# Attention values by token: transposes of the queries in place of a second projection

## What is computed

```python
qkv = x @ Wqkv_w.T + Wqkv_b
q = qkv[..., :nf]                      # nf = 192, 12 heads of 16
q = q.reshape(nb, ns, N_HEADS, hd).transpose(0, 2, 1, 3)
k = q
v = q
w = jnp.einsum('bhqd,bhkd->bhqk', q, k) * (1.0 / jnp.sqrt(jnp.float32(hd)))
mask = jnp.tril(jnp.ones((ns, ns), dtype=x.dtype))
w = jax.nn.softmax(w * mask - NEG_BIG * (1.0 - mask), axis=-1)
a = jnp.einsum('bhqk,bhkd->bhqd', w, v)
return a.transpose(0, 2, 1, 3).reshape(nb, ns, nf) @ Wproj_w.T + Wproj_b
```

## Time and profile before

| | us |
|---|---|
| median of three runs | 5412.71 |
| lowest, highest | 5407.25, 5437.77 |
| the profiled execution | 5446.25 |
| its span | 5444.5 |
| PE busy in it | 4705.0 (86%) |
| attention phase in it, about | 26 to 986 |

### The profile page before, as it was taken

One profiled execution on the slowest core, in us unless ns is written; L12 is line 12 of the kernel. 1 busy time (PEld: TensorE's weight loads), 2 busy tenths in 40 slices (PEclk: granted clock), 3 DMA queues, 4 the chain that ended last, 5 costly groups with the idle time before them and its releaser, 6 DMA issues. The chain is left out here.

```text
span 5444.5 us, 60695 instructions
## 1 busy us (share of the span) xinstructions
PE 4705.0 (86%) x16744; PEld 2469.9 (45%) x16744; DVE 3409.2 (63%) x4887; ACT 2337.0 (43%) x3842; POOL 3170.8 (58%) x1554
## 2 busy tenths in 40 slices
PE   5999999649959999999999898999899850899993
PEld 3777777326623433334434343434334320566662
DVE  2454544401119999999999999999999950111113
ACT  1333333302126566666666655566566530122220
POOL 2121111232219999999999898999899937222220
PEclk7999999869979999999999999999999975999996
DMA  4000000033312333332323232232233202333335
GB/s 192 16 15 12 15 15 6 13 94 120 104 45 97 103 105 104 104 103 101 105 96 112 88 102 97 98 107 96 97 100 105 90 13 77 117 112 114 114 113 166
DMA packets 239869, 473.51 MB, mean 87 GB/s; under 512 B 37324, under 2 KB 145180, under 8 KB 237692
## 3 DMA queue, kind: packets, MB, share of 16 engines
q1 hardware_dynamic: 216316, 424.11, 24.0%
q0 software_dynamic: 23424, 48.10, 2.5%
HBM read 399.02 MB, written 73.09 MB: 87 GB/s over the span
## 5 line engine op out<-in xcount | busy, mean ns | idle before, releaser
L1605 POOL TENSOR_TENSOR m_xh<-m_u,m_Bb 128x1536 f32<-128x1536 f32 x512 | 1760.9, 3467 | 203.4 <-DVE m_u L1483 203.4
L1534 PE MATMUL bank<-m_xh,ident 128*128 128x512 f32 x3072 | 1448.7, 607 | 24.6 <-POOL m_xh L1594 24.6
L1561 ACT ACTIVATE bank<-m_dt,m_Ac 128x508 f32<-128x508 f32 x1536 | 1020.9, 683 | 464.3 <-DVE bank L1576 310.0
L1576 DVE TENSOR_TENSOR_SCAN bank<-bank,m_xh 128x512 f32<-128x512 f32 x864 | 1059.5, 1226 | 34.1 <-ACT bank L1561 7.8
L1534 PEld LDWEIGHTS bank<-m_xh,ident 128*128 128x128 f32 x3072 | 570.8, 192 | 808.6 <-issue 730.9
L1594 POOL TENSOR_TENSOR m_xh<-m_xh,m_Cb 128x1536 f32<-128x1536 f32 x224 | 773.1, 3452 | 8.8 <-DVE m_xh L1576 8.8
L1576 DVE TENSOR_TENSOR_SCAN m_xh<-bank,m_xh 128x512 f32<-128x512 f32 x672 | 771.3, 1203 | 7.0 <-POOL m_xh L1605 3.6
L1585 DVE TENSOR_TENSOR m_xh<-bank,m_Cb 128x512 f32<-128x512 f32 x864 | 597.6, 692 | 66.8 <-DMA m_Cb<-BC_rows 21.2
L1017 POOL DMA_INDIRECT rows_y<-f1t_y,f1t_home x156 | 150.5, 965 | 565.2 <-DVE f1t_y L1046 527.7
L368 DVE TENSOR_REDUCE mx<-bank 128x3 f32<-128x384 f32 x256 | 142.3, 556 | 440.3 <-PE bank L535 439.2
L438 ACT ACTIVATE S<-S 128x384 f32<-128x384 f32 x256 | 133.9, 523 | 585.6 <-DVE S L370 585.6
(11 more groups left out here) (293 smaller groups left out, 6327.9 us busy)
## 6 DMA issues: line engine op xcount, KB each, us to landing
m_Bb<-BC_rows SPq DMA_DIRECT2D x256, 512.0 KB, 4.7
m_Cb<-BC_rows SPq DMA_DIRECT2D x256, 512.0 KB, 3.9
f1t_w<-f_w SPq DMA_DIRECT2D x39, 576.0 KB
slots_x<-zeros SPq DMA_DIRECT2D x12, 1254.5 KB, 31.1
f1t_x<-slots_x SPq DMA_DIRECT2D x39, 386.0 KB, 3.7
f1t_w1a<-f_w SPq DMA_DIRECT2D x39, 384.0 KB
f1c_yg<-rows_y SPq DMA_DIRECT2D x16, 768.0 KB, 4.7
f0t_w<-f_w SPq DMA_DIRECT2D x19, 576.0 KB, 4.4
```

The costliest lines, as they stand in the source:

```text
L1534: mm = pe.matmul(bank[:, c, :], K.ident[:, :], xh[n % NX][:, c, :], start=False, stop=(d == 1 and n == NS - 1))
L1561: act.activation(o[:, :, lo:hi], seqs(dt[d][:, c, :])[:, :, lo:hi], ACT.Exp, scale=Ac[:, c, n:n + 1]).then_inc(s_dA, 1)
L1576: dve.tensor_tensor_scan(o, bank[:, 3 + p % 3, way], xh[n % NX][:, c, way], 0.0, ALU.mult, ALU.add).then_inc(s_h, 1)
L1605: pool.tensor_tensor(xh[n % NX][:, :, :], u[d][:, :, :], Bb[q % RB][:, n % QN, :].unsqueeze(1).to_broadcast([P, DC, TOK]), ALU.mult).then_ ...
```

## The change

`V` is no longer computed by a second projection. The bias row of the padded weights gets a 1.0 in column 16 of each head, so that `qT` has a row of ones beside each head's 16 rows; transposing `qT` then gives the values, the ones column and the zeros at once. The projection has seven steps: k = 0, 1, 2 as before, and k = 3 to 6 one for each sequence, three 128x128 transposes of `qT` each, and one ScalarE copy of 128x384 each. k = 3 waits for all three copies of `qT`. The steps stand at other units. The weights `wq_a`, `wq_b` with their three loads go, and so do the four memsets of `V`; GpSimd gets one memset (twelve elements in one partition).

```diff
--- before.py
+++ after.py
@@ -143,7 +143,6 @@
         ds_t = sb("ds_t", [66, C])
         gam, bet = sb("gam", [P, C]), sb("bet", [P, C])
         wqp_a, wqp_b = sb("wqp_a", [P, HC * P]), sb("wqp_b", [CR + 1, HC * P])
-        wq_a, wq_b = sb("wq_a", [P, C]), sb("wq_b", [CR + 1, C])
         wo_a, wo_b = sb("wo_a", [P, C]), sb("wo_b", [CR + 1, C])
         mask = sb("mask", [P, HC, P], BF16)
         col_i = sb("col_i", [P, 2], I32)
@@ -184,7 +183,8 @@
         s_qps, s_q = sem("qps_ready"), sem("q_ready")
         s_sc, s_mx, s_sub, s_exp = sem("scores_ready"), sem("max_ready"), sem("sub_ready"), sem("exp_ready")
         s_pT, s_pTc, s_pv = sem("probsT_ready"), sem("probsT_copied"), sem("pv_ready")
-        s_OT, s_O, s_V = sem("heads_copied"), sem("heads_back"), sem("V_cleared")
+        s_OT, s_O = sem("heads_copied"), sem("heads_back")
+        NQ = HC + G
         s_ri, s_at, s_aT, s_aTc = sem("rowsum_inv"), sem("att_ready"), sem("attT_ready"), sem("attT_copied")
         s_pr, s_out = sem("proj_ready"), sem("res_ready")
 
@@ -203,20 +203,17 @@
                 pool.memset(mask[:, :, :], 0.0).then_inc(cleared, 1)
                 pool.iota(col_i[:, :], pattern=[[0, 2]], base=0, channel_multiplier=1).then_inc(cleared, 1)
                 pool.wait_ge(cleared, 4)
+                pool.memset(wqp_b[CR:CR + 1, :].rearrange("p (h x) -> p h x", x=32)[:, :, HD:HD + 1], 1.0).then_inc(cleared, 1)
+                pool.wait_ge(cleared, 5)
                 pool.affine_select(out=mask[:, :, :], in_=mask[:, :, :], compare_op=ALU.is_ge,
                                    fill=-4.0 * BIG, base=0, pattern=[[0, HC], [-1, P]], channel_multiplier=1).then_inc(cleared, 1)
-                pool.wait_ge(cleared, 5)
+                pool.wait_ge(cleared, 6)
                 pool.iota(col_i[64:128, 1:2], pattern=[[0, 1]], base=0, channel_multiplier=1).then_inc(cleared, 1)
-                pool.wait_ge(cleared, 6)
+                pool.wait_ge(cleared, 7)
                 pool.tensor_copy(col[:, :], col_i[:, :])
 
             @block.vector
             def _(dve):
-                for v in V:
-                    dve.memset(v[:, :, :, :], 0.0).then_inc(s_V, 1)
-                dve.wait_ge(s_V, 2)
-                for v in V:
-                    dve.memset(v[:, :, :, HD:HD + 1], 1.0)
                 dve.memset(zeros[:, :, :], 0.0).then_inc(s_zeros, 1)
                 dve.memset(mul3[:, :], 3.0).then_inc(mul3_set, 1)
                 dve.memset(zTb[CR:CR + 1, :], 1.0)
@@ -231,8 +228,6 @@
                 for dst, src in (
                     (posi_t[:, :], A["posi_table"]), (ds_t[0:64, :], A["demo_table"]), (ds_t[64:66, :], A["seg_table"]),
                     (gam[:, :], A["ln_gamma"].partition_broadcast(P)), (bet[:, :], A["ln_beta"].partition_broadcast(P)),
-                    (wq_a[:, :], A["WqkvT"][0:P, 0:C]), (wq_b[0:CR, :], A["WqkvT"][P:C, 0:C]),
-                    (wq_b[CR:CR + 1, :], A["bqkv"][0:1, 0:C]),
                     (wqp_a[:, :].rearrange("p (h x) -> p h x", x=32)[:, :, 0:HD],
                      A["WqkvT"][0:P, 0:C].rearrange("k (h d) -> k h d", d=HD)),
                     (wqp_b[0:CR, :].rearrange("p (h x) -> p h x", x=32)[:, :, 0:HD],
@@ -409,7 +404,7 @@
                 every_group(dve, dve_body)
 
 
-            Q_AT = {11: (0, 1), 13: (2, 3), 15: (4,)}
+            Q_AT = {11: (0, 1), 12: (2,), 14: (3, 4), 15: (5, 6)}
 
             def act_keep(act, g):
                 act.wait_ge(s_h1, g + 1)
@@ -417,7 +412,7 @@
 
             def act_zT(act, g):
                 if not isinstance(g, int) or g > 0:
-                    act.wait_ge(s_qps, g * 5)
+                    act.wait_ge(s_qps, g * NQ)
                 act.wait_ge(s_zTps, g * 2 + 1)
                 act.copy(zTa[:, :], bank[:, 6, :]).then_inc(s_zT, 1)
                 act.wait_ge(s_zTps, g * 2 + 2)
@@ -425,13 +420,11 @@
 
             def act_q(act, g, i, k):
 
-                act.wait_ge(s_qps, g * 5 + k + 1)
+                act.wait_ge(s_qps, g * NQ + k + 1)
                 if k < HC:
                     act.copy(qT[i][:, k, :], bank[:, 6 + k % 2, :]).then_inc(s_q, 1)
                 else:
-                    b = k - HC
-                    act.copy(V[i][:, 2 * b:2 * b + 2, :, 0:HD],
-                             bank[:, 6 + k % 2, 0:2 * C].rearrange("p (j h d) -> p j h d", j=2, h=HEADS)).then_inc(s_q, 1)
+                    act.copy(V[i][:, k - HC, :, :], bank[:, 6 + k % 2, 0:HC * P].rearrange("p (h d) -> p h d", h=HEADS)).then_inc(s_q, 1)
 
             def act_exp(act, g, u):
                 act.wait_ge(s_sub, g * UN + u + 1)
@@ -463,7 +456,8 @@
                     tile(act_OT, act, g, u, LC)
                     tile(act_aT, act, g, u, LA)
                     if u == 0 and not first(g):
-                        act_q(act, g, i, HC + 1)
+                        for k in Q_AT[UN - 1]:
+                            act_q(act, g, i, k)
                     if nxt is not None:
                         if u == 7:
                             act_keep(act, nxt)
@@ -477,7 +471,7 @@
             def _(act):
                 act_keep(act, 0)
                 act_zT(act, 0)
-                for k in range(HC + 2):
+                for k in range(NQ):
                     act_q(act, 0, 0, k)
                 every_group(act, act_body)
 
@@ -486,7 +480,7 @@
                 later = not isinstance(g, int) or g > 0
                 pe.wait_ge(s_onehot, g * 2 + 2)
                 if later:
-                    pe.wait_ge(s_q, g * 5)
+                    pe.wait_ge(s_q, g * NQ)
                 for b in range(2):
                     for j in (2 * b, 2 * b + 1):
                         o = bank[:, 6 + b, (j % 2) * C:(j % 2 + 1) * C]
@@ -505,28 +499,26 @@
                     mm = pe.transpose(bank[0:CR, 7, j * P:(j + 1) * P], z[:, j, P:C], K.ident[:, :])
                 mm.then_inc(s_zTps, 1)
 
-            def pe_q(pe, g, k):
+            def pe_q(pe, g, k, i):
                 if k == 0:
                     pe.wait_ge(s_zT, g * 2 + 2)
                 if k >= 2:
-                    pe.wait_ge(s_q, g * 5 + k - 1)
+                    pe.wait_ge(s_q, g * NQ + max(k - 1, HC if k == HC else 0))
                 if k < HC:
                     o = bank[:, 6 + k % 2, :]
                     pe.matmul(o, wqp_a[:, k * P:(k + 1) * P], zTa[:, :], start=True, stop=False)
                     pe.matmul(o, wqp_b[:, k * P:(k + 1) * P], zTb[:, :], start=False, stop=True).then_inc(s_qps, 1)
                 else:
-                    for j in (2 * (k - HC), 2 * (k - HC) + 1):
-                        o = bank[:, 6 + k % 2, (j % 2) * C:(j % 2 + 1) * C]
-                        sl = slice(j * P, (j + 1) * P)
-                        pe.matmul(o, zTa[:, sl], wq_a[:, :], start=True, stop=False)
-                        mm = pe.matmul(o, zTb[:, sl], wq_b[:, :], start=False, stop=True)
+                    j = k - HC
+                    for c in range(HC):
+                        mm = pe.transpose(bank[:, 6 + k % 2, c * P:(c + 1) * P], qT[i][:, c, j * P:(j + 1) * P], K.ident[:, :])
                     mm.then_inc(s_qps, 1)
 
             def pe_scores(pe, g, u, i):
                 j, r = u // RG, u % RG
                 n = g * UN + u
                 if u == 0:
-                    pe.wait_ge(s_q, g * 5 + HC)
+                    pe.wait_ge(s_q, g * NQ + HC)
                 if u >= 2 or not isinstance(g, int) or g > 0:
                     pe.wait_ge(s_sub, n - 1)
                 pe.matmul(bank[:, u % 2, 0:HC * P], K.identb[:, :], mask[:, :, :], start=True, stop=False)
@@ -548,8 +540,8 @@
                 j, r = u // RG, u % RG
                 n = g * UN + u
                 pe.wait_ge(s_pTc, n + 1)
-                if r == 0 and j % 2 == 0:
-                    pe.wait_ge(s_q, g * 5 + HC + j // 2 + 1)
+                if r == 0:
+                    pe.wait_ge(s_q, g * NQ + HC + j + 1)
                 if r == 0 and (j >= 2 or not isinstance(g, int) or g > 0):
                     pe.wait_ge(s_out, g * G + j - 1)
                 for c in range(HC):
@@ -595,14 +587,14 @@
                             pe_zT(pe, nxt)
                         elif u in Q_AT:
                             for k in Q_AT[u]:
-                                pe_q(pe, nxt, k)
+                                pe_q(pe, nxt, k, 1 - i)
 
             @block.tensor
             def _(pe):
                 pe_embed(pe, 0)
                 pe_zT(pe, 0)
-                for k in range(HC + 2):
-                    pe_q(pe, 0, k)
+                for k in range(NQ):
+                    pe_q(pe, 0, k, 0)
                 every_group(pe, pe_body)
```

## The result

The changed kernel took 5509.78 us (median of 22 runs, 5461.67 to 5558.73); the kernel before, measured beside it, 5454.96 us (22 runs). The ratio is 1.0098, with a 95% interval from 1.0069 to 1.0127: slower by 1%, or some 54 us. Every ratio here leaves out the few runs that lie over 1.5% above the fastest of their kernel, so it is not exactly the quotient of the two medians. The forecast was a ratio of 1.0035.

What follows compares the result with a forecast made beforehand. TensorE was taken to bound the attention phase; 5446.25 - 5.4 (start) + 24.2 (waits net of saved work) = 5465.1 us, factor 1.0035, applied to the 5412.71 us median: 5431 us. Own range 5412 to 5445; 8 in 10, 5389 to 5475.

Steps and rivals of the forecast that it cites:

- The bound, and 15 counts: Attention phase: TensorE is the bound, busy 137.02 of 140 us; the projections of groups 1 to 15 count 15 times.
- The start: Clears and loads before attention: without V's memsets 3.92 us and wq's loads 1.48 us, all that follows comes 5.40 us earlier.
- PE work: Projection steps: four transpose blocks, 1.52 us, replace 2.72 us of matmuls; gain 1.20 us per group, 18.0 us for 15.
- The hypothetical that the transposes are held at 1.2 GHz: New transpose blocks cost up to 3.04 us per group in place of 1.52; the gain becomes a loss, 5 us in all.
- The waits: PE waits for ScalarE copies, 1.03 us at u = 12 and 1.73 at u = 15; net +1.61 us per group, +24.2 us.
- Rival (a): The two copy waits are absorbed or not there: 5389 us without them, 5413 if absorbed; chance 0.18 for both.
- Rival (b), the clock: Clock falls in the u = 15 gap: 5509 us at one fall per group, 5440 to 5470 in a few; chance 0.17.
- the other row: Tail of the attention phase, 983 to 986 us: PE busy 1.20 of 3 us, next microsecond granted 0.80 on average.
- The price of a fall: Until the embedding at u = 1, two units take up to twice the time: 5.2 us per group, 78 us in all.
- The sum: Profiled execution: 5446.25 - 5.4 + 24.2 = 5465.1 us, a factor of 1.0035.
- The median: Whole kernel: the three runs' median, 5412.71 us, times the factor 1.0035 gives 5431.4 us.

Runs made afterwards that it cites:

- experiment 1: Changed kernel with ScalarE's qT and V copies at u = 12 and u = 15 put ahead of exp: ratio 0.9950, a second time 0.9948.
- the run with the long wait: Changed kernel with u = 15 copies early and the u = 12 wait lengthened to 2.1 us by two extra ScalarE copies: ratio 1.0034, again 1.0117.
- experiment 2: Changed kernel with only the copies at u = 12 ahead of exp, the wait at u = 15 left: ratio 1.0074.
- experiment 3: Changed kernel with only the copies at u = 15 ahead of exp, the wait at u = 12 left: ratio 0.9965.

## Why the prediction was wrong

- *The bound, and 15 counts*: right. The PE bounds the phase, and the waits stand 15 times each in the list.
- *The start*, -5.4 us: the mechanism right, mis-sized. 4.30 us at the slot clears, 3.52 where the PE waits for them, 2.1 at the `zTa` copy of group 1, behind the later rise of the clock. The forecast took the two parts as if nothing else in the chain moved.
- *PE work*, -1.20 us a group: right. By the starts of the rows a pair of blocks takes 0.71 and 0.77 us, 1.48 for the four against 2.72 before, a gain of 1.24. The period without the waits is 54.7 against 56.17 us, 1.4 to 1.5 less; what gives the other 0.2 was not looked for. The hypothetical that the transposes are held at 1.2 GHz, for which the prediction named the Trainium skill (TensorE: Matmul & The Clock Gate, Part 4: PE-mode transpose), did not come: experiment 1 ran them at 1.00.
- *The waits*, 1.03 and 1.73 us, +1.61 net: right. Measured in the same way 1.09 and 1.74, and +1.60. Reading where each copy stands in ScalarE's order, behind which exp, gave this to a few hundredths; the busy share of ScalarE (38% of the phase) would have given nothing.
- *Rival (a)*: refuted, no part of the waits was absorbed.
- *Rival (b), the clock*: this is the step that failed. The sum put the cost of the clock at nothing, where the runs show about 32 us. The rival had the place (the wait at u = 15), the direction and the rows, but a chance of 0.17, and most of that for "a few groups". The argument against it, "1.00 throughout from 160 to 300 us with the same transposes", compared a stretch without such idle spells with one that gets a spell of 1.7 us per group, and so was no argument. "A gap alone does not lower the clock" was too wide as well: the row from 2101 to 2104 us, where a longer gap (2.70 us) did no harm, lies between 512-column matmuls only, and the other row, the tail of the attention phase itself, was the nearest. It should have weighed most: it is the same mix of work. The Trainium skill (TensorE: Matmul & The Clock Gate, A second HAM failure mode: psum-queue depth-cycling) tells of a kernel in which short idle spells between groups of matmuls made the clock go back and forth; this case agrees for the waits of 1.0 to 2.1 us in the table, and not for the wait of 0.9 us at u = 12, which lowered nothing.
- *The price of a fall*, at most some 5 us before the embedding ends it: the size came out (61.4 us at half clock for six falls are 5 us each in the mean, 1.7 to 12 us one by one), the reason did not. In the changed kernel the falls of 3.4 and 6.8 us ended before the embedding began, and in the run with the long wait an embedding ran from 598.5 to 604.0 us and the clock stayed at 0.50 until 619. That the rival's 5509 us (one fall in every group, from a median of 5412.71) meets the measured 5509.78 is chance: the profile had six falls, and the kernel before had a median 42 us higher.
- *The sum*: 18.8 us forecast for the profiled kernel, 54.5 measured in the phase: -2 at the `zTa` copy of group 1 and +24 from the waits stand, about 32 from the clock were left out (21.9 in the fourteen periods and 10.7 behind them). Added, the forecast's ratio of 1.0035 becomes 1 + 50.8 / 5446 = 1.0093.
- *The median*: the absolute number was tied to three runs (5412.71); 22 runs of the same kernel gave 5454.96. Of the 78 us from 5431 to 5510 about 42 are that, and about 36 are the ratio. As ratios to 5412.71 the forecast's own range ends at 1.0060 and the wide one, for 8 in 10, at 1.0115: the measured 1.0098 is above the first and within the second, so the shift of the median alone carried the time out of the wide range. The mechanism that was forecast, waits and no fall of the clock, is refuted by the traces in either case.

## What to carry to other kernels

When an engine with a fixed order bounds a stage, price a moved step by what stands ahead of its supplier in the supplier's own order, not by the supplier's idle share; putting the supplier's copies at the head of their unit, ahead of its exp, turned +1% into -0.5%. And in a mix like this one (transposes, matmuls of 16 rows, products of 32 columns) an idle spell of one to two microseconds can cost several times its own length, as it may take the clock down for the next units (experiment 2: 25 us of waits, and 95.6 us at half clock, worth about 48); so remove it, or fill it with matmuls that nobody reads. That it is the narrowness of the work around the gap that matters is suggested by one row of another phase (2101 to 2104 us) and was not tested.

## What was not expected of the hardware

- After a fall, back-to-back work does not bring the clock back by itself in this mix: from 571 to 619 us the PE was busy 48.00 of 48 us and stayed at 0.50, through a whole embedding. Falls lasted from 10.2 to 47.8 us in that one execution, and from 3.4 us in others.
- More idle time did not mean more falls: 6 and 7 falls with two waits per group, 15 with the second alone.
- The first rise of the clock in the attention phase came at 123 us in the kernel before, at 132 and 119 us in two profiles of the same changed kernel, and at 85 us in that of experiment 3. Ten microseconds earlier or later are worth 5 us (an estimate, at half clock). In a single profile that hides a change: the phase of experiment 3 ends 3 us before that of experiment 1 (964 and 967 us), though its groups are 1.2 us longer, because its clock rose 47 us earlier.
